# An attention and mixture-of-experts block on one core: values projected two steps ahead, down projection one step later, routing from slot 0, straight code

## What is computed

```
x = x + attn(layernorm(x))
x = x + moe(layernorm(x))

attn: 16 heads, keys of 16, values of 64
  q, gates = split(x @ Wqg);  k, values = split(x @ Wkv)
  q, k, values = l2norm(q), l2norm(k), l2norm(values)
  a = square(relu(q k^T));   out = a @ values
  out = tanh(|out|) * out/|out| * tanh(silu(gates));  return out @ Wout

moe: 16 experts of width 64, top 4 of the best 2 of 4 groups, and one shared expert of width 128
  scores = sigmoid(x @ gate_kernel) + gate_bias
  group score = sum of its 2 best; keep 2 groups; top 4 of what is kept; weights = top / sum * 2.5
  y = sum_e weight_e * (silu(x @ w_gate_e) * (x @ w_up_e)) @ w_down_e
  return y + (silu(x @ sw_gate) * (x @ sw_up)) @ sw_down
```

## Time and profile before

| | us |
|---|---|
| median of 3 runs | 818.59 |
| profiled execution | 821.27 |
| span in its profile | 819.5 |
| TensorE busy, matmuls | 689.8 (84%) |
| VectorE busy | 524.8 (64%) |
| ScalarE busy | 435.0 (53%) |
| GpSimd busy | 352.6 (43%) |
| mean granted TensorE clock | 0.923 |

### The profile page before, as it was taken

The page is one execution under the profiler, slowest core; times in us unless marked ns, Lnnn a source line. Parts: engine busy times, 40 slices in busy tenths (PEclk is TensorE's granted clock), DMA queues, the critical chain, the costliest instruction groups (busy, mean ns, idle before and its releaser), DMA issues.

```text
span 819.5 us, 16266 instructions
## 1 busy us (share of the span) xinstructions
PE 689.8 (84%) x5160; PEld 544.4 (66%) x5160; DVE 524.8 (64%) x1739; ACT 435.0 (53%) x986; POOL 352.6 (43%) x368
## 2 busy tenths in 40 slices
PE   1576897988979797998979797997979798898785
PEld 1444475867767685876768585876768586776675
DVE  3446657576675758676675858667675856656654
ACT  2466765564645555564646556574656556443311
POOL 2235573544535254543535364443536353453100
PEclk9778998999989899998989999898999899898898
DMA  7995759092653819083561909174381909200000
GB/s 196 130 143 55 123 97 111 8 139 37 111 64 77 91 34 129 19 130 43 94 73 63 110 8 150 24 115 58 79 88 51 116 0 137 32 14 2 7 8 6
DMA packets 72801, 60.83 MB, mean 74 GB/s; under 512 B 8624, under 2 KB 72496, under 8 KB 72752
## 3 DMA queue, kind: packets, MB, share of 16 engines
q1 hardware_dynamic: 72752, 60.26, 49.7%
HBM read 41.37 MB, written 18.87 MB: 74 GB/s over the span
## 4 chain that ended last, share of the span: by engine, by line
PE 62%; DVE 24%; issue 6%; ACT 4%; DMA 2%; POOL 1%; SPq 1%; DVEq 0%; ACTq 0%; POOLq 0%
PE ps_a L508 12%; PE ps_f L370 9%; PE ps_f L433 7%; PE ps_f L372 7%; PE ps_f L371 7%; PE ps_f L452 5%; PE ps_s L479 5%; PE ps_f L429 4%; PE ps_f L412 3%; DVE norms_m L746 2%; DMA qkt<-qk_rows 2%; DVE norms_y L661 2%; PE ps_f L423 2%; DVE it L857 2%; DVE norms_t L666 2%
## 5 line engine op out<-in xcount | busy, mean ns | idle before, releaser
L339 POOL TENSOR_TENSOR p<-r 128x512 f32<-128x512 f32 x256 | 262.4, 1046 | 382.6 <-ACT r L608 382.6
L608 ACT ACTIVATE r<-ps_s 128x512 f32<-128x512 f32 x256 | 138.6, 597 | 81.4 <-PE ps_s L479 79.8
L508 PE MATMUL ps_a<-p,v 128*64 128x256 f32 x1024 | 143.5, 396 | 3.4 <-DVE big L902 2.2
L508 PEld LDWEIGHTS ps_a<-p,v 128*64 128x64 f32 x1024 | 64.5, 138 | 41.6 <-POOL p L339 2.6
L902 DVE TENSOR_TENSOR big<-ps_a,wt 128x256 f32<-128x256 f32 x128 | 53.6, 420 | 57.0 <-ACT big L617 56.0
L857 DVE TENSOR_TENSOR it<-ps_f,it 128x256 f32<-128x256 f32 x144 | 59.1, 420 | 40.7 <-ACT it L600 39.5
L600 ACT ACTIVATE it<-ps_f 128x256 f32<-128x256 f32 x144 | 55.2, 383 | 48.0 <-PE ps_f L372 45.8
L423 PE MATMUL ps_f<-ident,cs 128*32 128x128 f32 x32 | 9.2, 388 | 76.8 <-DVE cs L792 76.8
L452 PE MATMUL ps_f<-wdown,it 128*128 128x128 f32 x576 | 71.2, 279 | 2.9 <-DVE it L874 1.7
L874 DVE TENSOR_TENSOR it<-ps_f,it 128x512 f32<-128x512 f32 x64 | 44.0, 689 | 45.3 <-PE ps_f L429 44.7
L452 PEld LDWEIGHTS ps_f<-wdown,it 128*128 128x128 f32 x576 | 68.4, 195 | 4.5 <-DVE it L874 1.8
(11 more groups left out here) (153 smaller groups left out, 1606.7 us busy)
## 6 DMA issues: line engine op xcount, KB each, us to landing
qk_rows<-qk_parts SPq DMA_DIRECT2D x16, 1024.0 KB, 4.4
qkt<-qk_rows SPq DMA_DIRECT2D x64, 256.0 KB, 9.5
qkt<-qk_rows SPq DMA_DIRECT2D x128, 128.0 KB, 8.8
x_in<-in_L_attn_tokens SPq DMA_DIRECT2D x16, 128.0 KB, 2.2
x_res<-in_L_attn_tokens SPq DMA_DIRECT2D x16, 128.0 KB, 14.1
out<-o_sb SPq DMA_DIRECT2D x16, 128.0 KB, 14.0
big<-in_L_attn_Wqg SPq DMA_DIRECT2D x1, 640.0 KB, 4.2
big<-in_L_attn_Wkv SPq DMA_DIRECT2D x1, 640.0 KB, 5.6
```

The lines of the kernel that those rows point to most:

```text
L339: pool.tensor_tensor(p[h % 4][:], r[h % 2][:], r[h % 2][:], ALU.mult).then_inc(probs_done, 1)
L508: last = pe.matmul(ps_a[k % 2][64 * e:64 * e + 64, 0:N], v[q][:, t, h * DV:(h + 1) * DV], p[h % 4][:, t * N:(t + 1) * N], start=(t == 0), ...
L608: act.activation(r[h % 2][:], ps_s[h % 2][:], ACT.Relu).then_inc(relu_done, 1)
```

## The change

In the table of fillers:

- v moves from slots 0 and 1 (stage P) to slots 5, 6 and 7 (stage L): values are projected two steps ahead of their attention. `v` has three buffers, taken by block number mod 3, and the buffer `sq` of their squares has two parts in place of four; the four `sums` on VectorE move to slots 5 to 7.
- y2 moves from slots 6 and 7 (stage F) to slot 0 of the next step (a new stage D, block s-3). `output_rows` goes with it, to slot 0 on VectorE, and SyncE stores block s-3. There is one step more, 18.
- lg is the first entry of slot 0; `route_scores` and `route_groups` are in slot 0 on VectorE, `route_experts` at the start of slot 1. g comes in slots 1 to 4, one slot earlier for most; cB in slots 5 to 7, and `scale_hidden` with it.
- `normed_rows` of norm 1 goes to slot 3, xT to slot 4, `xl` to slot 4; the weights' low parts are made in slot 3 of step -2 (before, slot 5).
- The sums of squares transposed by nT have a buffer of their own (`n2row`); before they lay in `x1`, and ScalarE waited for `read["y2"]` there.
- `run_steps` is gone: all engines are straight code.

The core of the diff:

```diff
-        [("P", "v", 0), ("F", "lg", 0), ("P", "v", 1), ("F", "gu", 0), ("F", "gu", 1)],
+        [("F", "lg", 0), ("D", "y2", 0), ("D", "y2", 1)],
...
+        [("P", "g", 2), ("F", "gu", 5), ("F", "cT", 0), ("F", "gu", 6), ("O", "rT", 0)],
+        [("O", "rB", 0), ("O", "rB", 1), ("F", "gu", 7), ("O", "rB", 2), ("L", "xT", 0), ("O", "rB", 3), ("P", "g", 3),
+         ("F", "gu", 8)],
...
+        [("L", "qk", 1), ("F", "cB", 2), ("L", "v", 3), ("F", "cB", 3), ("O", "x2T", 0), SKIP],
...
-    OFFSET = {"L": 2, "P": 1, "N": 1, "A": 0, "O": -1, "F": -2}
+    OFFSET = {"L": 2, "P": 1, "N": 1, "A": 0, "O": -1, "F": -2, "D": -3}
...
-        v = [sb(f"v{q}", [P, T, HV]) for q in range(2)]
+        v = [sb(f"v{m}", [P, T, HV]) for m in range(3)]
...
-        sq = sb("sq", [P, 4 * 512])
+        sq = sb("sq", [P, 2 * 512])
...
                     load_qk(q)
-                if "F" in on:
-                    sp.wait_ge(read["y2"], (s - 1) * 2)
-                    sp.dma_start(out[s - 2].rearrange("(t p) d -> p t d", p=P), o_sb[:])\
+                if "D" in on:
+                    sp.wait_ge(read["y2"], (s - 2) * 2)
+                    sp.dma_start(out[s - 3].rearrange("(t p) d -> p t d", p=P), o_sb[:])\
                       .then_inc(out_stored, 16)
...
-            run_steps(pe, step)
+            run_flat(step)
...
                 def output_rows():
-                    wait(dve, out_stored, 16 * fb)
+                    db = s - 3
+                    wait(dve, out_stored, 16 * db)
                     for t in range(T):
-                        dve.wait_ge(done["y2"], 2 * fb + t + 1)
+                        dve.wait_ge(done["y2"], 2 * db + t + 1)
...
                     if k == 0:
                         gated_heads(k)
+                        if F:
+                            route_scores(link_f, fb)
                         if L_on:
...
                             row_stats(link_l, x_in[q], st1, mv1, var1)
                             link_l.end()
-                        if P_on:
-                            sums(0, s + 1)
-                            sums(1, s + 1)
+                        if F:
+                            route_groups(link_f)
+                        if "D" in on:
+                            output_rows()
+                    if k == 1:
+                        if F:
+                            route_experts(link_f, fb)
+                            link_f.end()
+                        gated_heads(k)
                         if F:
                             gate_up([0])
...
                         if L_on:
                             low_parts(1, s + 2)
                         if F:
-                            output_rows()
+                            scale_hidden([2])
+                        if L_on:
+                            sums(3, s + 2)
+                        if F:
+                            scale_hidden([3])
```

More of the change, by code:

```diff
@@ L62, in stages @@
         return on | {"N"} if on & {"P", "O"} else on
-    ALL = set(OFFSET)
-    FIRST_STEP, LOOP_FROM, LOOP_TO, LAST_STEP = -2, 4, B - 2, B + 1
-    assert all(stages(s) == ALL for s in range(LOOP_FROM - 1, LOOP_TO)) and (LOOP_TO - LOOP_FROM) % 2 == 0
+    FIRST_STEP, LAST_STEP = -2, B + 2
     with ExitStack() as ctx:
@@ L191, in bass_attn_moe_layer_kernel @@
         block = ctx.enter_context(nc.Block())
[L193 to L201, removed]
         def run_flat(step):
@@ L378, in filler @@
                 xb = q if stage == "L" else pb
-                if at is not None and kind in weights:
+                if at < 3 and kind in weights:
                     pe.wait_ge(w_lo, weights[kind])
@@ L578, in evacuate @@
                 elif kind == "ones":
-                    wait(act, read["y2"], 2 * (s - 2))
                     act.wait_ge(done[kind], count)
-                    act.activation(n2row[pq], ps[:, 0:N], ACT.Copy).then_inc(read[kind], 1)
+                    act.activation(n2row[:], ps[:, 0:N], ACT.Copy).then_inc(read[kind], 1)
                 elif kind in ("rT", "cT"):
@@ L908, in head_norm_roots, with residual_row @@
                         newton(link_norms, nt)
+                def residual_row(t):
+                    dve.wait_ge(done["y"], 2 * b + t + 1)
+                    dve.tensor_tensor(x1[pq][:, t, :], bank[("y", t)][:, 0:D], x_res[pq][:, t, :], ALU.add)\
+                       .then_inc(read["y"], 1)
                 for k in range(SLOTS):
@@ L941, in step @@
                         if F:
-                            gate_up([3])
+                            gate_up([2])
                         gated_heads(k)
                         if F:
-                            gate_up([4])
-                            route_experts(link_f, fb)
-                            link_f.end()
+                            gate_up([3, 4])
                     if k == 3:
@@ L987, in step @@
                                .then_inc(read["xT"], 1)
+                        if O:
+                            scale_heads([3])
                         if F:
-                            scale_hidden([2, 3])
-                    if k == 6:
+                            gate_up([8])
+                    if k == 5:
+                        gated_heads(k)
+                        if at == 0:
+                            expert_weights()
+                            dve.wait_ge(w_lo, 7)
                         if O:
                             dve.wait_ge(x_back[pq], (b - pq) * 8 + 16)
-                            for t in range(T):
-                                dve.wait_ge(done["y"], 2 * b + t + 1)
-                                dve.tensor_tensor(x1[pq][:, t, :], bank[("y", t)][:, 0:D], x_res[pq][:, t, :], ALU.add)\
-                                   .then_inc(read["y"], 1)
+                            residual_row(0)
+                        if L_on:
+                            sums(0, s + 2)
+                        if O:
+                            residual_row(1)
                             dve.wait_ge(read["y"], 2 * b + 2)
```

96 lines of the change are left out of this document (41 added, 55 removed), and 8 rows, old and new, of the table FILL.

## The result

The changed kernel takes **950.5 us** (median of four runs, 949.75 to 952.93) against 818.77 us for the kernel before (four runs, 818.45 to 820.5): a ratio of 1.161, with a 95% interval of 1.158 to 1.164, so 16% slower. The profiled execution took 950.28 us, its span is 948.2. The forecast was 921, in a range of 888 to 958.

What follows compares the result with a forecast made beforehand. TensorE, waiting 4.87 us in most steps for routing weights, was taken as the bound. Start 113.5, steps 2-3 41 + 43.1, steps 4-13 589, steps 14-18 52.3 + 33 + 25.5 + 24.2 gave 921 us, range 888 to 958.

Steps and rivals of the forecast that it cites:

- The term that decides it: Steps 4 to 14: VectorE's `output_rows` waits for the previous output store behind the loads; 58.9 us a step, 15.8 more than 43.1.
- The saving: Full steps: TensorE's 4.87 us wait on `cs` and the low-clock stretch go; 43.1 us a step without the store wait.
- the 3.2 us of small waits: TensorE's new waits in a step: rT about 0.5, slot 4 1.5, x2T in slot 7 1.15 us.
- C: Part of a step's loop from the store's release to the end of the next low_parts(1): 34.7 us.
- The start: Program start to step 2: 113.5 us against 119.5 before, bounds 108 to 121.
- The end: Last steps: step 14 52.3 us, step 15 33, step 16 25.5, step 17 with the added step 18 24.2.
- the slow stretch: TensorE's matmuls at the lower clock behind the `cs` idle time; 1.8 us, taken as 2.0 in a full step.
- The loops: PE, ACT and POOL lose a loop of five rounds over steps 4 to 13: costs nothing, bound 5 us either way.
- main case: The store wait paces steps 4 to 14 at 56.6 to 60.7 us: 890 to 950 us in all, chance 0.86.
- (a): Rival: the output store is served beside the loads and lands early, shift 4 to 5 us a step; 797 us, chance 0.05.
- (b): Rival: the store wait hides altogether and only the saving shows; 747 us, chance 0.03.
- (c): Rival: VectorE and GpSimd hinder each other more, steps of 62 to 65 us; 970 us, chance 0.06.

Runs made afterwards that it cites:

- Experiment 1: Changed kernel with the output store issued first in SyncE's step instead of last: 763.9 us, ratio 0.932 to the kernel before.
- Experiment 6: Experiment 1 with the split of the expert weights moved from slot 5 of step 0 to the end of step -1: 760.7 us.
- Experiment 5: Experiment 1 with VectorE doing `route_experts` before `output_rows` in steps 14 to 17: 761.4 us.
- experiment 3: Changed kernel with SyncE issuing the output store between the landing of the qk store and the first of the twelve loads: 763.9 us.
- experiment 2: Changed kernel with the output store issued from ScalarE's queue in slot 1 instead of by SyncE: 765.2 us.
- experiment 4: Kernel before with straight code on PE, ACT and POOL in place of the loop over steps 4 to 13: 824.6 us against 819.9.
- experiment 7: Experiments 5 and 6 together, on the changed kernel with the store first: 757.9 us, ratio 0.926 to the kernel before.
- experiment 8: Experiment 7 with v 3 and qk 1 exchanged in slot 7, and `sums(3)` with `low_parts(1)` on VectorE: 758.3 us.

## Why the prediction was right, point by point

The direction, the mechanism and the step's length came out as forecast; the total is 29.5 us (3%) above the 921, nearly all of it at the start and the end.

**The term that decides it.** The steps from 4 to 13 were put at 58.9 us and take 58.94. Both parts were near: from the qk store to the release 24.2 against a mean of 24.6 over the eleven turns (23.5 to 25.6), from the release to the next qk store 34.7 against 34.3 over the ten between them (34.0 to 35.0). VectorE was to arrive at 4.85 us of the step: in step 4 it begins to wait at 226.90 - 17.02 = 209.88, 4.84 us behind the logits at 205.04. The eleven waits are 16.8 to 18.9 us, inside the 15 to 19 given, and 198 us in all for the 190. They stand in steps 4 to 14 and nowhere else, as laid out. Experiment 1 shows the cause and not only the size: with the store's place in SyncE's order changed, and nothing else, the wait is absent and the step is 42.2 us.

**The saving.** The `cs` wait is gone, and the step without the store wait, put at 43.1 us, is 42.20. The two parts of the 43.1 miss in opposite directions: in experiment 1 TensorE is busy 40.3 us of a step and not 39.8 (400.85 of the 420 us from 200 to 620), and of the 3.2 us of small waits only some 1.8 show: x2T 0.95 of 1.15, rT 0.7 of 0.5, slot 4 0.15 of 1.5. I had laid slot 4 out with VectorE behind its whole queue, and it is further ahead than that. C, in which the same 1.5 us were counted, came out 0.4 too long.

**The start: 113.5 us predicted, 122.94 measured, a term too short by 9.4.** The qk store of block 0 is 2.07 us later (24.12), as laid out with 2.4. The rest of that term fails: it held that the expert weights are better covered. The timeline of TensorE and VectorE in step 0, against the earlier trace rows:

```profile
48.18 0.80 PE L464 MATMUL ps_s<-qkt 64*128 64x256 f32 x4 [6.66 <-DMA qkt<-qk_rows]
...
67.04 0.66 PE L370 MATMUL ps_f<-ident,xn 128*128 128x128 f32 x2 [2.54 <-DVE xn L668]
...
75.92 1.36 DVE L705 TENSOR_TENSOR weg_lo<-big,weg_hi 128x1152 fp32r<-128x1152 f32 x1 [3.42 <-ACT weg_hi L522]
```

Scores come only 0.6 us later than before. But the split of the expert weights stands in slot 5, in front of the values and `qk` that now fill slots 5 to 7 on ScalarE and VectorE: more waits behind it, not less. Experiment 6 takes it away and gets about 4.2 of the 9.4 us. No run isolated the other 5; one piece that the rows show is in step 0, where TensorE waits 2.54 us for VectorE's first normalisation.

**The end: steps 14 to 18 put at 135.0 us, measured 153.8.** Step 14 is over by 2.9, 15 by 5.6, 16 by 2.6, and the last stretch by 7.7. In steps 14 to 16 the step of the sum that failed is the same, and in the last stretch it is a part: I took the `cs` wait and the slow stretch, 6.7 us, off each, and put almost nothing in its place. Windows of step 15, of the kernel before and then of experiment 1, where no store wait disturbs it:

```profile
724.80:763.60 38.80, 33.73 (x263) 26.36 (x261) 23.83 (x86) 16.09 (x40) 16.98 (x17) 0.91 0.02 6
```

```profile
667.20:704.40 37.20, 33.31 (x263) 24.56 (x261) 26.90 (x86) 15.77 (x39) 16.98 (x17) 1.00 0.03 8
```

Equal work, 263 matmul instructions in both. The step was to lose 6.7 us and gain 1; it loses 1.6. TensorE's idle time falls only from 5.1 to 3.9 us, since small waits take the place of the one on `cs` (1.1 us at x2T, 0.8 at rT, 0.6 at cT for its bank, 0.8 at a projection), and the higher clock shortens the busy time by 0.4 us and not 1.8. In its last step the kernel before had only 3.12 us of the wait on `cs`:

```profile
803.38 0.38 PE L423 MATMUL ps_f<-ident,cs 128*32 128x128 f32 x2 [3.12 <-DVE cs L792]
```

so 1.8 us of the 6.7 were never there. And block 14's down projection, which I priced at 4.1 us, runs partly at the lower clock, as the timeline of the changed kernel shows (the first row is an earlier one of the same size), and the window around it:

```profile
850.12 4.26 PE L437 MATMUL ps_f<-wdown,it 128*128 128x128 f32 x36
...
917.12 7.09 PE L437 MATMUL ps_f<-wdown,it 128*128 128x128 f32 x36
```

```profile
916.00:930.00 14.00, 12.06 (x74) 11.89 (x75) 6.57 (x37) 2.12 (x7) 0.00 (x0) 0.76 0.03 10
```

That is 2.8 us more for the same 36 matmuls. The routing behind it, which I took to lie beside it, comes after: the output rows are at 924.24 and the experts' last instruction at 926.80. Experiment 5 buys 1.2 us of that in the last stretch. A part of the end belongs to the changed kernel alone: step 15 takes 38.6 us in it at a mean clock of 0.96 and 37.2 in experiment 1 at 1.00, the last stretch 31.9 at 0.79 and 29.6 at 0.88. That is 3.8 of the 18.8 us.

**The loops.** "Nothing, bound 5 us either way" was 4.7 us in the kernel before. It is inside the bound, and the value taken was wrong; the evidence stood in the earlier trace rows, where a straight step has 5.01 us of wait and a looped one 4.87. The rule of the Trainium skill, Runtime: NRT & Kernel Launch, Instruction fetch mechanics, by which straight code would gain, does not show in this kernel: straight code was 0.6% slower.

**The sum.** The 921 are 29.5 us too short, and 26.6 of them are in the span: 9.4 from the start, 18.8 from the end, less 1.6 from steps 2 to 13 (39.9, 42.2 and 589.4 for 41, 43.1 and 589). Two small regions of the program, where I scaled the old durations and did not lay the order out, hold all of this. The other 2.9 us come from the steps between span and median: I took 2.7 off because the profiled execution before lay that much above the median, and here it does not. That the total stayed in the range owes something to luck: start and end were given -8 to +10 and are 28.2 over, and 950.5 lies just outside the 890 to 950 of the main case. It fits because the loops, given -25 to +20, were hit almost exactly.

**The rivals.** (a), the store lands early, is refuted: in the changed kernel the stores land after 13.6 us in the median. Its price exists, 1.8 us, but only ahead of the loads (experiment 3), and a queue of its own does not bring it (experiment 2). The Trainium skill, DMA: Bandwidth & Descriptors, Anatomy of one DMA, gives the fixed cost that the prediction sets beside (a) for DMAs that GpSimd issues, and for one DMA by itself; so the 14.0 us behind the loads do not test it. (b), the wait hides, is refuted by the eleven waits; its 747 us is what a kernel without them would have reached by my sum, and 763.9 is what it reached. (c), engines hindering each other, named steps of 62 to 65 us; the longest is 60. The total came out between the main case and (c) for another reason, start and end.

Not tried: a second `o_sb` buffer, which would let the output rows go ahead without waiting for the last store.

## What to carry to other kernels

When work moves across a step boundary, look up every semaphore it waits for, then find where the signal's issuer stands in its own in-order queue and what that is held by: here the store's turn in SyncE's order, and not its size, cost 17 us in each of eleven steps, and moving three lines turned 16% slower into 7% faster. Price such a wait as a loop, from the event that starts the chain to the release and from the release back to that event; here the two parts were 0.4 us off each, in opposite directions, and the loop 0.04. Lay out start and end step by step with the same care: they held the error of the span here, and what a cleared wait gives there is often taken by the next one.

## What the runs showed of the hardware

- A 128 KB store lands in 1.8 us ahead of twelve loads (median, experiment 3), in 14.1 us behind them (experiment 1), and in 14.0 us from another engine's queue, when it is issued 5 us after the first of them (experiment 2).
- In the kernel before, straight code on three engines was 4.7 us (0.6%) slower than a loop of five rounds (experiment 4), with a wait of 5.00 us for one of 4.87.
- TensorE's clock at the end of the program differed between the profiled executions of two kernels that differ little: the mean granted clock of step 16 was 0.94 in experiment 7 and 0.83 in experiment 8, 2.5 us longer for the same matmuls. What tips it was not isolated.
- VectorE instructions of 0.24 us or less lasted 0.96 to 0.98 us where they met a GpSimd squaring (changed kernel, 528 to 535 us). `split_hi`, a copy to another type with one input, is among them.
